# Layer 1 attention: q, k and v projected turned, in two halves each, with the rotary rows exchanged by DMA, and weight work moved into the stages ahead

## The reference, cut to what matters

```python
q, k, v = proj(wq), proj(wk), proj(wv)            # (x @ w.T), split into 16 heads
q1r = q1 * cos + rotate_half(q1) * sin            # the first 16 of 32 channels
k1r = k1 * cos + rotate_half(k1) * sin
att = softmax(q @ k.T / sqrt(32)); y = att @ v
```

## Time and profile before

| what | us |
|---|---|
| median of 3 runs (lowest, highest) | 3008.83 (3008.29, 3011.52) |
| the profiled execution, its span | 3014.07, 3012.3 |
| PE busy | 2851.8 (95%) |
| DVE busy | 1857.4 (62%) |
| ACT busy | 1292.5 (43%) |
| POOL busy | 1412.6 (47%) |
| mean granted TensorE clock | 0.981 |

### The profile page before, as it was taken

One profiled execution on the slowest core, in us unless ns is written; L12 is line 12 of the kernel. 1 busy time (PEld: TensorE's weight loads), 2 busy tenths in 40 slices (PEclk: granted clock), 3 DMA queues, 4 the chain that ended last, 5 costly groups with the idle time before them and its releaser, 6 DMA issues. The chain is left out here.

```text
span 3012.3 us, 54363 instructions
## 1 busy us (share of the span) xinstructions
PE 2851.8 (95%) x19392; PEld 2012.1 (67%) x19392; DVE 1857.4 (62%) x2724; ACT 1292.5 (43%) x2021; POOL 1412.6 (47%) x1000
## 2 busy tenths in 40 slices
PE   7999999699999996799999999999999789999999
PEld 5878787578888885555555555555555368888887
DVE  5656766566777763666666666666666744444444
ACT  3221111266666663255555555555555532222222
POOL 2103556122323322277777777777777732222222
PEclk9999999899999998799999999999999999999999
DMA  3211111112222223222222222222222332222221
GB/s 126 88 61 49 61 64 52 36 50 102 86 84 91 97 81 124 102 71 71 71 71 71 71 71 71 71 71 71 71 71 70 134 120 90 84 84 90 90 84 49
DMA packets 124567, 238.99 MB, mean 79 GB/s; under 512 B 13440, under 2 KB 48384, under 8 KB 124416
## 3 DMA queue, kind: packets, MB, share of 16 engines
q1 hardware_dynamic: 120896, 235.32, 23.6%
q10 hardware_dynamic: 3520, 1.46, 0.2%
HBM read 178.02 MB, written 58.72 MB: 79 GB/s over the span
## 5 line engine op out<-in xcount | busy, mean ns | idle before, releaser
L1286 DVE TENSOR_REDUCE l_attn_maxima<-l_attn_ps_max 128x2 f32<-128x1024 f32 x502 | 613.2, 1222 | 234.9 <-PE l_attn_ps_max L1414 230.8
L1257 POOL TENSOR_TENSOR l_attn_summed<-l_attn_summed,l_attn_probs 128x1024 f32<-128x1024 f32 x248 | 585.8, 2397 | 51.2 <-ACT l_attn_probs L1195 51.2
L1195 ACT ACTIVATE l_attn_probs<-l_attn_ps_sc 128x1024 f32<-128x1024 f32 x512 | 497.6, 1029 | 158.0 <-PE l_attn_ps_sc L1402 131.2
L1257 POOL TENSOR_TENSOR l_attn_summed<-l_attn_probs 128x1024 f32<-128x1024 f32 x124 | 293.7, 2391 | 241.5 <-ACT l_attn_probs L1195 241.5
L1662 POOL TENSOR_TENSOR l_ffn_ht_lo<-l_ffn_mixed,l_ffn_ht_hi 128x512 fp32r<-128x512 f32 x88 | 114.0, 1296 | 414.2 <-ACT l_ffn_ht_hi L1683 414.2
L62 PE MATMUL l_attn_ps_prep<-l_w_tile,l_x_tiles 128*128 (+1 forms) x1440 | 286.1, 347 | 6.4 <-DVE l_attn_qk_lo L1280 2.1
L1424 PE MATMUL l_attn_ps_y<-l_attn_probs,l_attn_v 128*32 128x512 f32 x2048 | 273.2, 606 | 1.1 <-ACT l_attn_probs L1195 1.1
L62 PEld LDWEIGHTS l_attn_ps_prep<-l_w_tile,l_x_tiles 128*128 128x128 f32 x1440 | 247.8, 189 | 39.0 <-issue 29.1
L71 PE MATMUL l_ffn_ps_fc<-l_ffn_t_fc,l_ffn_ct_hi 128*128 128x512 f32 x512 | 213.4, 417 | 7.0 <-DVE l_ffn_ct_lo L823 3.6
L71 PE MATMUL l_ffn_ps_out<-l_ffn_t_proj,l_ffn_ht_hi 128*128 128x512 f32 x512 | 206.1, 402 | 0.0
L71 PE MATMUL l_ffn_ps_fc<-l_ffn_t_fc,l_ffn_ct_lo 128*128 128x512 f32 x512 | 203.8, 398 | 0.0
(11 more groups left out here) (270 smaller groups left out, 6522.0 us busy)
## 6 DMA issues: line engine op xcount, KB each, us to landing
l_x_tiles<-xt_chunks SPq DMA_DIRECT2D x160, 512.0 KB, 4.0
xt_chunks<-l_ffn_xt SPq DMA_DIRECT2D x32, 512.0 KB, 4.4
l_attn_xin<-in_x SPq DMA_DIRECT2D x32, 256.0 KB, 4.3
l_attn_piece<-in_w_fcT SPq DMA_DIRECT2D x16, 512.0 KB, 4.3
s<-l_attn_s_sb SPq DMA_DIRECT2D x32, 256.0 KB, 2.2
l_attn_piece<-in_w_projT SPq DMA_DIRECT2D x16, 512.0 KB, 3.8
l_ffn_xa<-in_x SPq DMA_DIRECT2D x32, 256.0 KB, 2.7
l_ffn_xb<-in_x SPq DMA_DIRECT2D x32, 256.0 KB, 2.9
```

The source lines that it names most:

```text
L1195: act.activation(probs[kt % RING][:, hs, :], ps_sc[:, hs, :], ACT.Exp, scale=ATT_SCALE).then_inc(exp_done, 1)
L1257: pool.tensor_tensor(total[:, hs, :], old[:, hs, :], probs[kt % RING][:, hs, :], ALU.add).then_inc(added, 1)
L1286: dve.tensor_reduce(maxima[b][:, j, PAIR * hp:PAIR * hp + PAIR, half:half + 1], pair, AX.X, ALU.max).then_inc(max_read, 1)
```

## The change

- **Projection turned.** w is now the stationary side (128 columns of q, k or v) and four chunks of x (512 tokens) the moving one. q, k and v of half a unit are three products of 12 matmuls of 512 columns, each in two parts of six in two steps running (`project_half`). q and k come out turned, so their turns go. v comes out turned too, and is turned back (`turn_v`).
- **Rotary.** The channels lie on partitions now. ACT copies the product to `plain`; SP exchanges rows of eight partitions by eight DMAs, `plain` to `exchanged` (`swap`); DVE multiplies the product in PSUM by the cosine table (`by_cosine`), `exchanged` by the sine table (`by_sine`), adds them (`rope_sum`); ACT rounds the sum (`rounded`), DVE subtracts (`low_half`).
- **Places in the tick.** A half has eight steps: parts of q in steps 0 and 1, k in 2 and 3, v in 4 and 5, "max" in 6, v's turn and "den" in 7; the other half the same from step 8. Cosine comes two steps after a half's first part, sine and sum three, rounding and low four.
- **Loads.** x is loaded four chunks at a time, behind v's half (`load_half`). A table of 128x2x1024 comes in at the start.
- **No loop.** All ticks of layer 1 attention are written out (`every`).
- **Stages ahead.** The layer 0 FFN has no block of its own ahead: ACT and DVE expand the fc codes at its start, ACT and POOL the proj codes in ticks 0 and -1. Its last ticks load and split the group 0 weights of layer 1 and load four chunks of x, so that layer 1 attention starts with both. Buffers are shared to make room: the probabilities and the last FFN's small tiles lie in `stage`.

```diff
+        HALF_AT = {0: ("q", 0), 2: ("k", 0), 4: ("v", 0), 8: ("q", 1), 10: ("k", 1), 12: ("v", 1)}
+        EVENTS = {6: ("max", 1, 0), 7: ("den", 2, 0), 14: ("max", 1, 1), 15: ("den", 2, 1)}
+        V_TURNS = {7: 0, 15: 1}
...
+        COS_AFTER, SIN_AFTER, SUM_AFTER, HI_AFTER, LO_AFTER = 2, 3, 3, 4, 4
...
+            for t in range(1, NT + 2):
+                tick(t, t % 2)
...
+            def swap(t, s):
+                if half_at(t, s):
+                    sp.wait_ge(proj_read, reads_by(t, s) - 1)
+                    need(sp, rope_step, rope_by(turned_by(t, *half_at(t, s)) - 1))
+                    for n in range(HPG):
+                        for a in range(2):
+                            to, of = (HD * n + R // 2 * x for x in (a, 1 - a))
+                            sp.dma_start(exchanged[to:to + R // 2, :], plain[of:of + R // 2, :]).then_inc(swap_in, 16)
...
+            def by_cosine(t, kind, h):
+                dve.tensor_tensor(roped[kind], ps_prep[:, :, :]..., turn_tabs[:, 0, DIM * h:DIM * h + DIM], ALU.mult).then_inc(proj_read, 1)
+            def by_sine(t, kind, h):
+                need(dve, swap_in, 16 * 2 * HPG * (n - 6))
+                dve.tensor_tensor(exchanged, exchanged, turn_tabs[:, 1, DIM * h:DIM * h + DIM], ALU.mult).then_inc(rope_step, 1)
+            def rope_sum(t, kind, h):
+                dve.tensor_tensor(roped[kind], roped[kind], exchanged, ALU.add).then_inc(rope_step, 1)
+            def low_half(t, p, kind, h):
+                dve.tensor_tensor(qk_lo[p][:, a, cols], roped[kind], fp32(qk_hi[p][:, a, cols]), ALU.subtract).then_inc(lo_ready, 1)
...
-                    first, rest = ((0, 1), (2, 3)) if s % 2 else ((0,), (1, 2, 3))
+                    first, rest = ((0, 1), (2, 3)) if s in (7, 15) else ((0,), (1, 2, 3))
...
+            def project_half(t, s, part):
+                for k in range(KD // 2 * part, KD // 2 * (part + 1)):
+                    for w, x in ((w_hi, 0), (w_hi, 1), (w_lo, 0)):
+                        mm = pe.matmul(ps_prep[:, :, :], cols(w, k), x_tiles[:, :, x, k, :], ...)
...
+            def expand(n):
+                pool.tensor_copy(t_proj[:, PIECE * n:PIECE * (n + 1), :], proj_codes[:, PIECE * n:PIECE * (n + 1), :]).then_inc(proj_expanded, 1)
```

More of the change, by code:

```diff
@@ L597, in layer0_ffn @@
         codes = two("codes", [P, DIM])
-        ct_hi, ct_lo = two("ct_hi", [P, KD, P], F32R), two("ct_lo", [P, KD, P], F32R)
+        small = lambda first, count: [w_tile[:, KD * FC + DIM * (first + i):KD * FC + DIM * (first + i + 1)].rearrange("p (k n) -> p k n", k=KD) for i in range(count)]
+        ct_hi, ct_lo = small(0, 2), small(2, 2)
         h = [stage[:, FC * i:FC * (i + 1)] for i in range(2)]
@@ L980, in layer1_attention @@
+                if s - 1 in HALF_AT and half_at(t, s - 1):
+                    return proj_read, reads_by(t, s - 1)
+                if event(t, s):
+                    kind, m, i = event(t, s)
+                    return {"max": (max_t_ready, QB * m + i + 1), "den": (den_read, QB * m + i + 1)}[kind]
+                if v_turn(t, s):
+                    return v_ready, v_turns_by(*v_turn(t, s)) + 1
         HALF = CPB // 2
@@ L1045, in early_pair, with turned_by, rope_by, qk_half @@
             return ps_sc[:, 0:PAIR, :] if i <= LAST_QB0 and i % 2 == 0 else ps_max[:, :, :]
-        sched = (1, 2, NT, NT + 1)
+        def turned_by(t, kind, h):
+            return TURNS * t + 1 + 2 * h + "qk".index(kind)
+        def rope_by(n):
+            return 2 * n + 4 * EARLY - 12
+        def qk_half(t, s, after):
+            half = half_at(t, s - after) if s >= after else None
+            return half if half and half[0] != "v" else None
+        def hi_at(t, s):
+            return qk_half(t, s, HI_AFTER)
+        def every(tick):
+            for t in range(1, NT + 2):
+                tick(t, t % 2)
         @block.sync
@@ L1127, in _ @@
             prologue()
-            ticks(sp, *sched, tick)
+            every(tick)
             for b in range(2):
                 sp.wait_ge(y_den_stored[b], 32 * NT)
-            sp.wait_ge(x_ahead, 16 * CHUNKS // CPB)
+            for b in range(XTS):
+                sp.wait_ge(xt_ld[b], 16 * (CPB // XTS) * NT)
+            sp.wait_ge(swap_in, 16 * 2 * HPG * (4 * NT - 6))
         @block.scalar
@@ L1218, in _ @@
             prologue()
-            ticks(act, *sched, tick)
+            every(tick)
         @block.gpsimd
@@ L1259, in _ @@
             remainders()
-            ticks(pool, *sched, tick)
+            every(tick)
         @block.vector
@@ L1382, in _ @@
             prologue()
-            ticks(dve, *sched, tick)
+            every(tick)
         @block.tensor
@@ L1538, in _, with layer1_ffn @@
             prologue()
-            ticks(pe, *sched, tick)
-def layer1_ffn(nc, x1_in, xt_in, yt_in, den_in, downT, s_gate, s_up, s_down, out, x_tiles, w_tile, wo_hi, wo_lo):
+            every(tick)
+def layer1_ffn(nc, x1_in, xt_in, yt_in, den_in, downT, s_gate, s_up, s_down, out, x_tiles, w_tile, wo_hi, wo_lo, stage):
     x1_t = x1_in.rearrange("(c p) d -> c p d", p=P)
@@ L1557, in layer1_ffn @@
         sc_gate, sc_up, sc_down = sb("sc_gate", [P, KH]), sb("sc_up", [P, KH]), sb("sc_down", [P, DIM])
-        yt, den = two("yt", [P, GROUPS, P]), two("den", [P, GROUPS, P])
+        yt, den = [stage[:, DIM * (14 + i):DIM * (15 + i)].rearrange("p (g n) -> p g n", g=GROUPS) for i in range(2)], two("den", [P, GROUPS, P])
         xt_ld = sem("xt_ld")
```

363 lines of the change are left out of this document (240 added, 123 removed).

## The result

The changed kernel takes **3143.83 us** (median of 4 runs, 3140.08 to 3147.14) against 3010.18 before (4 runs, 3008.29 to 3013.82): **ratio 1.0439, interval 1.0424 to 1.0453**, slower. The forecast was 3031, with a range to 3080: the sign was right and the size was off by a factor of six. The profiled execution took 3147.14 (span 3145.4, granted clock 0.962).

The account below looks back on a forecast made before the run. TensorE, busy 95% of the span, was taken to bound the kernel through its order in layer 1 attention. Terms 41 - 8 - 6 - 4 = +22 gave 3036 profiled, 3031 us median; range 2960 to 3080.

Parts of the forecast that it names:

- My layout: Layer 1 attention: DVE's two-SBUF-input operations wait for GpSimd's adds; tick 75.8 against 72.9, +41 us; chance 0.50.
- The exchange by DMA: Each half of layer 1 attention: eight DMAs, issue 0.33 each, landing 2.5 later, ahead of both sines.
- my scale: Times in us from the start of half a tick, as laid out step by step; the half ends at 38.2.
- Rival 2: Exchange comes late: one add more in front of sine, 2 us a half, 28 halves, +50, 3080; chance 0.12.
- The clock, put at nothing inside the ticks: TensorE's clock falling in other stretches (half and full levels show at the edges) would move edge terms some us.
- PE alone: Layer 1 attention by TensorE's slots only: tick 69.8 against 72.9, a gain of 3.1 us a tick.
- the cosine's 0.3 a step: With no wait between DVE and GpSimd, only this delay remains: half 35.7, tick 71.0, -27 us.
- the 0.5 that I took off: Slots for the old tick gave 73.4 against 72.9 in the trace, so 0.5 per tick was subtracted.
- den's store, which waits a step or two for nobody: SP's list in layer 1 attention: the exchanges stand ahead of this store, taken to delay nobody.
- The signs: Sine, sum, low: median above 1 us, most above 2.5; tick near 76; PE idle before maxima in steps 4, 7.
- Edges and loop: Layer 0 FFN edge -6, layer 1 edge -4, writing out the loop's six returns of 1.4 us idle -8.
- the 7.6 of the prediction: Layer 0 FFN edge: SP issues the first load at block entry, so the chain moves 7.6 us earlier.

Follow-up runs that it names:

- Two tiles: Changed kernel with one tile for q's exchanged rows and another for k's, so k's exchange need not wait for q's sum: 3079.28 us (1.0219).
- the control without adds: Kernel before with ticks written out and GpSimd's adds cut to 128x16 in units 1 to 14: 3001.24 us (0.9965).
- repaired: Changed kernel with the rotary sum on GpSimd and weight loads ahead of the denominators' store, single exchange tile: 2989.49 us (0.9918).

## Why the prediction was wrong

- **"My layout", right as a mechanism.** DVE's two-input operations wait for GpSimd's adds, and the reduces behind them hold PE. Without adds a tick falls from 82.3 to 72.3. Where the exchange is in time, the tick is 76.0 (75.8 forecast). The prediction named a rule of the Trainium skill for this (SBUF — State Buffer, "SBUF: two separate sides"): VectorE with two SBUF inputs and GpSimd share a pair of ports, which one instruction holds to its end. It is borne out: 58 cosines with one operand in PSUM never took over 0.69.
- **The step that failed: "The exchange by DMA".** I took SP's issue at 0.33 from a load of x. It is 0.66 for these: 5.3 us for eight and not 2.7. The landing was taken 2.5 behind the last issue and is 1.4, so that 1.1 of the 2.6 came back. k's exchange lands at 26.5 of my scale and not at 25. k's sine then meets a whole add (2.68, not 0.68), and step 6 takes 7.1, not 3.9. Two tiles remove that alone and give 65 us. Rival 2 named this lateness, but at q's sine and as one add a half, 50 us.
- **A second part of the same term.** q's sine meets one add more in 7 of the 29 halves of the changed kernel and in 8 of 29 with two tiles (8.2 to 10.0 us for the step). In some of them a single issue takes up to 1.5 us in place of 0.62; in the others the sine waits for a landing up to 2.5 us behind the last issue in place of 1.4. What holds them isn't settled. With two tiles a tick is 78.0 on average and 76.0 without such a half: 28 us in 14 ticks.
- **The clock, put at nothing inside the ticks.** I had named only the edges. It fell behind PE's waits in the middle of ticks. Of the 132 us that ticks 2 to 15 take more than without adds, 80 are PE's idle time and 52 are PE busy for longer with the same work at 0.95 of the clock. So by estimate some 50 us are the clock's. No run keeps the waits and changes the clock alone, so this is no more than an estimate.
- **"PE alone", mis-sized.** With only the cosine's 0.3 a step left, the prediction has 71.0; 72.3 was measured without adds (72.1 in eight ticks without the exchange too). That a second part follows the maximum by 0.24 was wrong: it follows by 0.42 (1592.04 to 1592.46), as the first does, so the odd steps take 4.37 and not 4.23. And the 0.5 that I took off was too much: my slots for the kernel before (6 x 3.60, 2 x 4.68, 8 x 5.17, 4 x 0.2) add up to 73.1 and not to 73.4. So the 75.8 of the layout was hit partly by luck: its PE slots are too short by 1.3 a tick, and its waits for GpSimd too long by 1.1 (75.8 less 71.0 laid out; 76.0 less 72.3 measured).
- **"den's store, which waits a step or two for nobody", wrong.** The loads of the FFN's weights wait behind it in SP's list: 17.5 us. The prediction moved den's event by five steps and did not ask what stands behind its store in the last ticks.
- **Put together**: 65 for k's sine, 28 for q's late halves and 17.5 for the tail are 110 of the 113 us between 3031 and 3143.8. The clock's share is inside the first two.
- **The signs.** sine (median 2.06) and sum (1.71) showed the wait, but no sum came near 2.5, and low took 1.12 behind q and 0.68 behind k in most halves. PE waited ahead of the second maximum of step 4, as forecast, and of the first of step 6, not 7. DVE idle until a DMA in front of sine, the sign of rival 2, was there 54 times in 58. Both were true at once.
- **Edges and loop, right.** The edges: forecast -6 and -4.4, measured -6.3 and -4.5 by the rows, and -11.4 together in the runs. The loop: forecast -8.4, measured -11.8. SP's first load of the FFN went out 3.2 us behind DVE's last add of layer 0 attention (578.54 to 581.75), where it was 10.8 (575.60 to 586.39): the 7.6 of the prediction.
- **The prologue and tick 1** have 3.3 us that I gave no term (107.7 against 104.4). With the sum on GpSimd they take 104.2 and 104.6 at the same granted clock of 0.84, and DVE is busy for 68.5 and 69.1 us in them, not 73.6: so the 3.3 go with DVE's waits, as in the ticks behind. In other profiles the clock adds to it. The old projection takes 104.4 and 104.0 at 0.81 and 0.82, but 107.7 at 0.77 (the control without adds) and 107.5 at 0.79 (edges and loop alone).

## What to carry to other kernels

Before an operation is added to VectorE, look at where its operands lie. With two in SBUF, and GpSimd adding beside it, count the wait for a whole add, and lay GpSimd's list out so that it waits for such an operation rather than runs beside it. Price each DMA of a new kind at more than the nearest one, and let its margin be larger than that error. When an event moves, read every queue for what stands behind the instruction that waits for it, the last ticks included. Count a wait of PE at more than its length where the clock falls behind it. Here the best parts of the change were the plain ones (loop and edges, 0.9927), and the new projection, even repaired (0.9918), is no faster than they are: the intervals overlap.

## What the runs showed of the hardware

- An exchange of 8 partitions by 512 columns between SBUF places (16 KB) took SyncE 0.62 us to issue (median of 464), one every 0.67. A 512 KB load from DRAM took 0.33 in the kernel before. The last of eight landed 1.4 us behind the end of its issue.
- An operation that starts earlier need not end earlier: q's sine started 0.86 us earlier behind its cosine, took 1.72 in place of 0.86, and ended at the same 7.53, since it fell into the middle of an add.
- The wait works both ways. Four adds took 10.30 us in a stretch with two such operations, 2.58 each, where they took 2.36 before.
- Behind an idle of 1.93 us in the middle of a stage PE's granted clock fell from full to half (0.53 from 1616.00 to 1618.59). With PE idle for 14.3 us in two ticks it was 0.96 on average, with 4.2 it was 1.00.
- A wait of PE cost more than its own length here: with two tiles PE was idle for 20 us less in ticks 2 to 15 and busy for 40 us less, at a clock of 0.99 in place of 0.95.
